# Cross attention: the negated maxima as two rows of the turned queries, by way of DRAM; gate logits with the gate as the stationary side

## The chip, the cores and the metric

The kernel runs on one core of a Trainium2 chip. The time is the device time of one execution, in microseconds. The engines are named as the profile names them: PE is TensorE (PEld its weight loads), DVE is VectorE, ACT is ScalarE, POOL is GpSimd, and SP issues most DMAs.

## What is computed

The program is one block of a model with two layers, for 4 batches of 512 tokens with 512 features (16 tiles of 128 tokens). The change lies in the second layer, in its cross attention and in the routing of its mixture of experts. Cut to those two:

```
# cross attention: 16 heads of 32 features, in 4 groups of 4 heads that share keys and values
scores = einsum('bghsd,bgtd->bghst', qh, kh) / sqrt(32)
probs  = softmax(scores, axis=-1)
out    = einsum('bghst,bgtd->bghsd', probs, vh)      # back to (b, s, 512)
x      = x + tanh(g_xattn[1]) * (out @ Wc.T + bc)
# mixture of experts: 8 experts, two for each token
gate_logits = einsum('bsd,de->bse', layernorm(x), gate_kernel)    # 512 -> 8, in f32
top_k_weights, top_k_indices = top_k(gate_logits, 2)
x = x + tanh(g_ffn[1]) * (weighted sum of the two experts)
```

The queries are the layer norm of x; the keys and values are both the context, 512 positions with 4 groups of 32 features.

## The kernel before

The kernel is written engine by engine: each engine has its list of instructions, and semaphores order them across engines. There is no scheduler. The stages follow one another: first attention, first feed-forward part, cross attention (functions with `_c`), routing (`_route`), experts (`_slots`).

**Cross attention.** It runs over 16 tiles `i` of 128 queries, and in each over 16 steps `s`; `k = 16 i + s`. A step does two different things for two different tiles.

- `scores(n)` makes the 128x512 scores of tile n // 16 and head n % 16, queries down and keys across, and DVE's `peak(n)` takes the maximum of each row. This runs ahead of the rest by `LEAD` = 24 steps.
- `scores_t(k)` makes the scores once more, turned: 128 keys down, 4 heads times 128 queries across, one product of 512 columns for group `g` and key block `c`. The maximum of each query has to be taken off before the exponential, and it varies across the columns here. So DVE's `split(i)` cuts the negated maxima into three bf16 parts in four small steps, PE's `mturn(i)` turns them, DVE's `spread_max(i)` spreads them into a tile `RM` of 128x512, and each `scores_t` begins with a product of a matrix `sel` of zeros and ones with `RM` into the same bank. ACT's `exps(k)` then makes the exponential into a ring of 12 buffers (`PT`).
- `values(k)`, two at every second step and four steps behind, multiplies by the values in f32, each call on 32 of PE's columns.
- POOL's `pool_sums` adds the exponentials of the four key blocks of a group, three additions for four steps, for the sums of the softmax.

The 32 features of a head fill only a quarter of PE's 128 rows. So the queries are laid out in four parts of 32 columns a head, two f16 high and two f16 low ones, and the keys too (`parts`, `twins`, `doubled`), which gives all four partial products in one matmul. `queries(i, half)` turns them on PE, ACT's `qcopy` copies them to `QTH`.

Behind the steps of tile `i` the previous tile is finished: `sums`, `sums_turn`, `spread_turn` (PE), `invert`, `normalise` (DVE), and `project` with 13 products. All of these, the query turns and `mturn` share PSUM bank 7, so their order on PE, and waits between them, keep them apart. Two banks (3 and 4) take the turned scores: `scores_t(k)` waits for the exponential of step k - 2.

**Routing.** For each of 16 tiles DVE normalises 512 features (`prep`), ACT makes their f16 high part (`high`), DVE the low one (`low`), PE turns the tile in four 128x128 f32 pieces (`turn`), ACT copies them (`zcopy`), and PE multiplies (`logits`): the stationary side is a turned piece of 128x128, the moving side 128x8 of the gate, four times a tile. There are two buffers of each kind, and the middle tiles run in a loop. Some fifty small steps of DVE on the logits follow, and then the experts. SP's loads of the first expert's weights wait for the first logits.

## Time and profile before

| | us |
|---|---|
| median of 3 runs | 1933.1 (1927.11 to 1937.12) |
| the profiled execution, its own time | 1933.01 |
| its span | 1931.2 |
| PE busy | 1554.0 (80%) |
| DVE busy | 1128.5 (58%) |
| ACT busy | 988.3 (51%) |
| POOL busy | 646.9 (33%) |
| PE's granted clock, mean | 0.893 of full |

The page cuts the span into 40 equal slices of 48.3 us, with the busy share of each engine and PE's granted clock in tenths. A table of windows gives the same for stretches of one's choice. The timeline gives each instruction, or a run of the same ones, with start, duration, line, operation and shape, and in square brackets how long the engine had been idle and who released it. A matmul's duration includes its way through the array; what it costs PE is the distance to the next one's start.

### The profile page before, as it was taken

The numbers are of one execution on the slowest core, as the hardware profiler recorded it, in microseconds if no ns is written. First come the engines' busy times: TensorE is split into PE (matmuls) and PEld (weight loads), VectorE is DVE, ScalarE is ACT, GpSimd is POOL, SyncE is SP. The second block draws the span as 40 slices with busy tenths as digits, with TensorE's granted clock in tenths as the row PEclk, the third lists the DMA queues.
The fourth block names the chain that finished last, engine by engine and source line by source line (L and its number), as shares of the span: only waits on it lengthen the run. The fifth ranks groups of instructions, "written<-read, shape, count | busy, mean of one in ns | idle before, by whom it ended". The sixth has DMA issues, their size and how long they took to land. (4 is left out here: it accounts for less than half of the span.)

```text
span 1931.2 us, 31926 instructions
## 1 busy us (share of the span) xinstructions
PE 1554.0 (80%) x10646; PEld 820.5 (42%) x10647; DVE 1128.5 (58%) x1845; ACT 988.3 (51%) x1487; POOL 646.9 (33%) x562
## 2 busy tenths in 40 slices
PE   6666565767677766999999780599999999999994
PEld 2444454533333332444444380244444444444442
DVE  3999999788888887777777354405145050522000
ACT  4999999522222224766766432144444443444442
POOL 3000000110000002777777606444445453444342
PEclk9777878788988887999999955799999999999998
DMA  9311100000000000000000036514255151532113
GB/s 333 122 44 44 44 1 1 28 1 0 0 0 0 0 1 1 2 2 2 2 2 2 18 136 256 201 34 122 64 163 163 33 158 27 163 79 51 28 24 102
DMA packets 48415, 118.45 MB, mean 61 GB/s; under 512 B 4736, under 2 KB 4992, under 8 KB 47744
## 3 DMA queue, kind: packets, MB, share of 16 engines
q1 hardware_dynamic: 34000, 88.26, 13.5%
q0 software_dynamic: 8176, 18.65, 5.0%
q10 hardware_dynamic: 6144, 10.28, 1.8%
q8 instruction: 58, 0.95, 0.2%
q14 instruction: 37, 0.30, 0.0%
HBM read 84.08 MB, written 37.30 MB: 63 GB/s over the span
## 5 line engine op out<-in xcount | busy, mean ns | idle before, releaser
L1608 PE MATMUL PS<-R 128*128 (+1 forms) x1872 | 432.8, 381 | 8.6 <-issue 7.5
L1762 DVE TENSOR_SCALAR R<-wring 128x1024 f16<-128x1024 f32 x56 | 61.4, 1107 | 383.0 <-PE PS L1631 349.5
L423 ACT ACTIVATE R<-R 128x512 bf16<-128x512 f32 x448 | 278.4, 710 | 9.9 <-DVE R L528 3.5
L1608 PEld LDWEIGHTS PS<-R 128*128 128x128 f16 x1872 | 179.3, 98 | 218.2 <-issue 20.4
L443 PE MATMUL PS<-R,ident_b 128*128 128x256 bf16 (+1 forms) x1056 | 161.6, 312 | 87.5 <-ACT R L423 83.6
L1631 PE MATMUL PS<-R 128*128 (+1 forms) x936 | 214.8, 379 | 1.2 <-ACT R L1718 1.2
L1023 DVE TENSOR_REDUCE R<-PS 128x1 f32<-128x512 f32 x256 | 167.8, 686 | 76.4 <-PE PS L1213 74.9
L1798 POOL TENSOR_TENSOR R<-R 128x512 f32<-128x512 f32 x78 | 113.5, 1456 | 292.4 <-ACT R L1706 181.1
L868 PE MATMUL PS<-R 128*128 128x512 bf16 x512 | 143.8, 433 | 77.1 <-DVE R L804 57.6
L1145 ACT ACTIVATE R<-PS 128x512 f32<-128x512 f32 x256 | 150.8, 597 | 86.3 <-PE PS L1228 85.2
L1000 POOL TENSOR_TENSOR R<-R 128x512 f32<-128x512 f32 x128 | 168.5, 1316 | 32.8 <-ACT R L1145 18.7
L443 PEld LDWEIGHTS PS<-R,ident_b 128*128 128x128 bf16 x1056 | 111.0, 117 | 116.8 <-ACT R L423 93.4
L321 POOL TENSOR_TENSOR rstd<-vare,mhalf 128x15 f32<-128x15 f32 (+1 forms) x8 | 13.2, 1658 | 365.1 <-DVE vare L308 337.4
L1631 PEld LDWEIGHTS PS<-R 128*128 128x128 f16 x936 | 89.9, 98 | 102.6 <-issue 1.4
L1806 POOL TENSOR_TENSOR R<-R 128x512 f16<-128x512 f32 x78 | 98.6, 1264 | 79.0 <-ACT R L1712 79.0
L626 POOL TENSOR_TENSOR R<-C,R 128x512 f16<-128x512 f32 x8 | 11.2, 1418 | 331.0 <-ACT R L621 331.0
L941 ACT ACTIVATE R<-PS 128x512 f32<-128x512 f32 x64 | 38.2, 597 | 159.8 <-PE PS L868 159.8
L1712 ACT CAST R<-R 128x512 f16<-128x512 f32 x78 | 48.2, 618 | 137.9 <-POOL R L1789 71.8
L1702 ACT ACTIVATE R<-PS 128x512 f32<-128x512 f32 x78 | 46.6, 597 | 140.0 <-PE PS L1608 140.0
L997 POOL TENSOR_TENSOR R<-R 128x512 f32<-128x512 f32 x64 | 89.5, 1398 | 79.6 <-ACT R L1145 77.9
L868 PEld LDWEIGHTS PS<-R 128*128 128x128 bf16 x512 | 52.3, 107 | 149.0 <-DVE R L804 79.6
L1718 ACT COPY R<-PS 128x1024 f16<-128x1024 f16 x78 | 79.0, 1012 | 58.3 <-PE PS L1620 58.3
(262 smaller groups left out, 2727.2 us busy)
## 6 DMA issues: line engine op xcount, KB each, us to landing
wring<-in_L_ffn_w_kernel_dram SPq DMA_DIRECT2D x48, 512.0 KB, 5.0
slot_rows<-R SPq DMA_DIRECT2D x1, 10023.0 KB, 40.1
R<-slot_rows ACTq DMA_DIRECT2D x39, 257.0 KB, 2.7
R<-in_L_ffn_w_kernel_dram SPq DMA_DIRECT2D x16, 512.0 KB, 6.0
wring<-in_L_ffn_wo_kernel_dram SPq DMA_DIRECT2D x16, 512.0 KB, 4.7
R<-in_L_ffn_wo_kernel_dram SPq DMA_DIRECT2D x16, 512.0 KB, 4.7
X<-in_x_dram SPq DMA_DIRECT2D x4, 1024.0 KB, 10.1
R<-in_L_ffn_w_up_dram SPq DMA_DIRECT2D x4, 1024.0 KB, 10.3
```

The lines of the kernel that those rows point to most:

```text
L423: nc.scalar.activation(marks[:, j * S:(j + 1) * S], SIM[:, tile * S:(tile + 1) * S], ACT.Sign, bias=cfloat[:, tile:tile + 1], scale=-1.0). ...
L443: mm = nc.tensor.matmul(bank[4 + h % 2][:, lo * 64:hi * 64], weight, marks.rearrange("p (t m) -> p t m", m=S)[:, lo:hi, c * 64:(c + 1) * 6 ...
L868: mm = nc.tensor.matmul(bank[2 * m + n], bzt[b][:, k * P:(k + 1) * P], WGU[:, col:col + 512], start=(k == 0), stop=(k == 3))
L997: nc.gpsimd.tensor_tensor(to, PT[u * 4 % RINGP], PT[(u * 4 + 1) % RINGP], ALU.add).then_inc(sx_step, 1)
L1000: nc.gpsimd.tensor_tensor(to, to, PT[(u * 4 + c) % RINGP], ALU.add).then_inc(sx_step if c == 2 else sx_done, 1)
L1023: nc.vector.tensor_reduce(cmx[:, n % NH:n % NH + 1], bank[n % 3], AX, ALU.max).then_inc(max_done, 1)
L1145: nc.scalar.activation(PT[k % RINGP], bank[3 + k % 2], ACT.Exp, scale=QK_SCALE).then_inc(exp_done, 1)
L1608: mm = nc.tensor.matmul(bank[2 * half + g], ZT[n][:, (4 * pz + k) * P:(4 * pz + k + 1) * P], weights(place, at), start=(i % 12 == 0), stop ...
L1631: mm = nc.tensor.matmul(bank[4], ITT[half][:, (4 * pz + c % 4) * P:(4 * pz + c % 4 + 1) * P], weights(place, at), start=(half == 0 and i = ...
L1718: nc.scalar.copy(ITT[half], bank[6 + half].bitcast(F16)).then_inc(itt_sb, 1)
L1798: nc.gpsimd.tensor_tensor(IT[half], SL[half], U[half], ALU.mult).then_inc(it32, 1)
L1806: nc.gpsimd.tensor_tensor(IL[half], IT[half], IH[half], ALU.subtract).then_inc(il_sb, 1)
```

## The change

**In the cross attention** the product with `sel` goes, and `sel`, `RM`, `mask` and `spread_max` with it. The negated maxima enter the scores themselves. The fourth part of the keys is now a constant: 8.0 in its first two columns and zeros elsewhere; the fourth part of the queries is zero. So `scores` sees three of the four partial products and nothing from part four. DVE's `split` makes -maximum/8 as an f16 high and an f16 low part, in two steps. PE's `mturn` turns those 32 columns, a new `max_copy` on ACT copies the 32x128 result, and a new `sp_maxima` on SP writes it to a small DRAM tensor and reads it back as 2 rows of 2048 into rows 96 and 97 of `QTH[i % 3]`, behind the last `scores` of that tile. `scores_t` then waits for that transfer in place of `rm_done` and is a single product.

`LEAD` becomes 28. The work around the steps is moved: query turns from s = 0, 2 to 1, 3, `mturn` from 10 to 5, `sums` from 4 to 6, `sums_turn` from 6 to 8, `spread_turn` from 8 to 10; `project` does 9 of its products at 13 and 4 at 15. ACT and DVE follow. DVE's subtraction for the query parts works on 512 columns instead of 1024. In the key preparation POOL does one subtraction a batch instead of two, and two fills once.

**In the routing** the gate is the stationary side, 128x32 (8 columns, the rest zeros), and a turned tile the moving side. Four tiles are done together, each on its own 32 of PE's columns; the 128x128 result, logits down and tokens across, is copied by DVE, turned back by PE (`back`), and after the last one DVE copies all logits at once. Buffers of each kind become four, and the loops are written out. POOL's tables and SP's expert loads wait for the first four tiles' logits instead of the first tile's.

```diff
-        LEAD, LAG, RINGP = 24, 4, 12
+        LEAD, LAG, RINGP = 28, 4, 12
+        KEY_ONE = 8.0
...
+        def sp_maxima(sp):
+            for i in range(NT):
+                sp.wait_ge(mq_sb, i + 1)
+                if i > 1:
+                    sp.wait_ge(max_in, (i - 1) * 16)
+                sp.dma_start(MD[i % 2][:, :], mq).then_inc(mq_out, 16)
+                sp.wait_ge(mq_out, (i + 1) * 16)
+                sp.dma_start(QTH[i % 3][96:98, :], MD[i % 2][:, :].rearrange("(n h) q -> n (h q)", n=2)).then_inc(max_in, 16)
...
-                nc.vector.tensor_tensor(twins(qs, 1), doubled(cz), twins(qs, 0), ALU.subtract).then_inc(qlo, 1)
+                nc.vector.tensor_tensor(parts(qs, 2), heads(cz), parts(qs, 0), ALU.subtract).then_inc(qlo, 1)
...
+            def max_copy(i):
+                act.wait_ge(mt_ps, i + 1)
+                if i:
+                    act.wait_ge(mq_out, i * 16)
+                nc.scalar.copy(mq, bank[7].bitcast(F16)[0:32, 0:P]).then_inc(mq_sb, 1)
...
             def scores_t(k):
                 i, g, c = k // NH, k % NH // 4, k % 4
-                pe.wait_ge(rm_done, i + 1)
+                pe.wait_ge(max_in, i * 16 + 16)
...
-                nc.tensor.matmul(to, sel[:, g * P:(g + 1) * P], RM[i % 2], start=True, stop=False)
-                nc.tensor.matmul(to, KTA[:, at:at + P], QTH[i % 3][:, g * 512:(g + 1) * 512], start=False,
+                nc.tensor.matmul(to, KTA[:, at:at + P], QTH[i % 3][:, g * 512:(g + 1) * 512], start=True,
                                  stop=True).then_inc(st_ps, 1)
...
                     if s == 13 and i:
-                        if i + 1 < NT:
-                            pe.wait_ge(rm_done, i + 2)
-                        else:
-                            pe.wait_ge(rcp_sb, i)
-                        project(i - 1)
+                        pe.wait_ge(rcp_sb, i)
+                        project(i - 1, ((0, 0), (0, 1)))
+                    if s == 15 and i:
+                        project(i - 1, ((1, 0),))
...
                 for k in range(4):
-                    mm = nc.tensor.matmul(bank[2 + b][:, 0:NE], dzt[b][:, k * P:(k + 1) * P],
-                                          GK[:, k * NE:(k + 1) * NE], start=(k == 0), stop=(k == 3))
+                    for j in range(4):
+                        mm = nc.tensor.matmul(bank[4 + q % 2][32 * j:32 * j + 32, 0:P], GK[:, k * 32:(k + 1) * 32],
+                                              dzt[j][:, k * P:(k + 1) * P], start=(k == 0), stop=(k == 3))
                 mm.then_inc(lg_ps, 1)
```

PE in a middle tile of the cross attention, steps 4 to 6 before. L1227 is the product with `sel`, L1228 the turned scores, L1213 the scores for the maxima, L1246 the sums, L1238 the values, L1252 a turn for the sums:

```order
L1227 MATMUL PS<-R 128x512
L1228 MATMUL PS<-R,wring 128x512
L1213 MATMUL PS<-wring,R 128x512
L1246 MATMUL PS<-R,ones 32x512 x4
L1227 MATMUL PS<-R 128x512
L1228 MATMUL PS<-R,wring 128x512
L1213 MATMUL PS<-wring,R 128x512
L1238 MATMUL PS<-R,C 32x128 x8
L1227 MATMUL PS<-R 128x512
L1228 MATMUL PS<-R,wring 128x512
L1213 MATMUL PS<-wring,R 128x512
L1252 MATMUL PS<-ident,R 128x128 x4
```

The same engine now, steps 5 to 8. L1232 is the turned scores, L1218 the scores for the maxima, L1242 the values, L1223 the turn of the maxima, L1250 the sums, L1256 the turn for the sums:

```order
L1242 MATMUL PS<-R,C 32x128 x8
L1223 MATMUL PS<-ident_h,R 32x128
L1232 MATMUL PS<-R,wring 128x512
L1218 MATMUL PS<-wring,R 128x512
L1250 MATMUL PS<-R,ones 32x512 x4
L1232 MATMUL PS<-R,wring 128x512
L1218 MATMUL PS<-wring,R 128x512
L1242 MATMUL PS<-R,C 32x128 x8
L1232 MATMUL PS<-R,wring 128x512
L1218 MATMUL PS<-wring,R 128x512
L1256 MATMUL PS<-ident,R 128x128 x4
```

A step has two products of 512 columns instead of three, and the turn of the maxima stands just ahead of the sums, which were at step 4.

PE in the routing before, the first tiles and the loop's body. L1527 is a tile's turn, L1535 its logits; the other rows belong to the loop:

```order
L1527 MATMUL PS<-ident,R 128x128 x8
L1535 MATMUL PS<-R 128x8 x4
L1542 UNCONDITIONAL_BRANCH
L1542 ISA
L1525 REGISTER_ALU
L1527 MATMUL PS<-ident,R 128x128 x4
L1531 REGISTER_ALU
L1535 MATMUL PS<-R 128x8 x4
```

The same place now; L1533 is the turns, L1542 the logits of four tiles, L1548 the turn back:

```order
L1533 MATMUL PS<-ident,R 128x128 x24
L1542 MATMUL PS<-R 32x128 x16
L1533 MATMUL PS<-ident,R 128x128 x12
L1548 MATMUL PS<-ident,R 128x128
L1533 MATMUL PS<-ident,R 128x128 x4
L1542 MATMUL PS<-R 32x128 x16
```

Six tiles' turns stand ahead of the first logits instead of two, and the logits come once for four tiles.

## Rows read from the trace of the kernel before

**Rows 1.** The page: busy tenths of PE and POOL, and PE's clock, in forty slices.
```profile
PE   6666565767677766999999780599999999999994
...
POOL 3000000110000002777777606444445453444342
PEclk9777878788988887999999955799999999999998
```

**Rows 2.** Table of windows: busy us (instructions) of each engine, PEclk, DMA share, GB/s.
```profile
775.00:1050.00 275.00, 274.27 (x2817) 129.05 (x2819) 208.48 (x343) 190.52 (x306) 207.44 (x154) 1.00 0.01 2
...
1110.00:1150.00 40.00, 39.53 (x192) 39.34 (x192) 20.70 (x47) 17.77 (x32) 2.21 (x9) 0.50 0.46 169
```

**Rows 3.** Timeline of PE, two steps: start, duration, line, operation, shapes, count.
```profile
882.18 0.38 PE L1227 MATMUL PS<-R 128*128 128x512 bf16 x1
882.39 0.38 PE L1228 MATMUL PS<-R,wring 128*128 128x512 f16 x1
...
882.92 0.64 PE L1238 MATMUL PS<-R,C 128*32 128x128 f32 x16
883.50 0.39 PE L1227 MATMUL PS<-R 128*128 128x512 bf16 x1
...
884.15 0.61 PE L1203 MATMUL PS<-ident_h,R 128*128 128x128 f16 x8
```

**Rows 4.** Timeline of PE: projections of two tiles, twelve tiles apart.
```profile
789.52 2.75 PE L1268 MATMUL PS<-R 128*128 128x512 f16 x12
...
1050.52 2.75 PE L1268 MATMUL PS<-R 128*128 128x512 f16 x12
```

**Rows 5.** Timeline of POOL: an addition held up, and two groups without a gap.
```profile
899.48 1.89 POOL L997 TENSOR_TENSOR R<-R 128x512 f32<-128x512 f32 x1 [1.12 <-ACT R L1145]
...
1074.83 2.69 POOL L1000 TENSOR_TENSOR R<-R 128x512 f32<-128x512 f32 x2 [2.25 <-ACT R L1145]
...
1079.06 2.69 POOL L1000 TENSOR_TENSOR R<-R 128x512 f32<-128x512 f32 x2
```

**Rows 6.** Timeline of ACT: a copy of half the turned queries, and two exponentials.
```profile
882.38 1.01 ACT L1138 COPY R<-PS 128x1024 f16<-128x1024 f16 x1
...
1074.15 1.09 ACT L1145 ACTIVATE R<-PS 128x512 f32<-128x512 f32 x2 [4.05 <-PE PS L1228]
```

**Rows 7.** Timeline of PE: the sums of the last tile.
```profile
1095.19 1.06 PE L1246 MATMUL PS<-R,ones 128*32 128x512 f32 x8 [1.66 <-POOL R L1000]
```

**Rows 8.** Timelines of PE, ACT and DVE at the start of the cross attention.
```profile
748.58 0.29 PE L1218 MATMUL PS<-ident_b,R 128*128 128x128 bf16 x1 [1.10 <-ACT R L1138]
...
753.11 0.63 PE L1227 MATMUL PS<-R 128*128 128x512 bf16 x1
...
748.42 1.24 ACT L1128 ACTIVATE R<-X,nmr,rstd 128x1024 f16<-128x1024 f32 x1
...
729.82 1.23 DVE L1017 TENSOR_TENSOR R<-R 128x1024 f16<-128x1024 f32 x1
```

**Rows 9.** The page, DMA issues: queue, count, KB each, us from issue to landing.
```profile
R<-in_L_xattn_Wq_dram SPq DMA_DIRECT2D x1, 64.0 KB, 5.8
...
R<-n_L_ffn_gate_kernel_dram ACTq DMA_DIRECT2D x1, 16.0 KB, 1.9
```

**Rows 10.** Timelines of PE, ACT and DVE in the routing.
```profile
1110.47 1.94 PE L1527 MATMUL PS<-ident,R 128*128 128x128 f32 x8 [3.87 <-DVE R L1389]
...
1113.96 1.09 PE L1527 MATMUL PS<-ident,R 128*128 128x128 f32 x4
1114.85 1.71 PE L1535 MATMUL PS<-R 128*128 128x8 f32 x8
1116.42 1.09 PE L1527 MATMUL PS<-ident,R 128*128 128x128 f32 x4
...
1115.84 0.58 ACT L1507 COPY R<-PS 128x512 f32<-128x512 f32 x1
...
1150.20 0.17 DVE L1400 COPY R<-PS 128x8 f32<-128x8 f32 x1 [1.54 <-PE PS L1535]
```

More of the change, by code:

```diff
@@ L1176, in act_c @@
             high(2)
+            max_copy(0)
             for i in range(NT):
@@ L1259, in spread_turn, with project @@
                 mm.then_inc(rst_ps, 1)
-            def project(i):
+            def project(i, parts):
                 pe.wait_ge(cot_hi, i + 1)
-                nc.tensor.matmul(bank[7], one_h, bch, start=True, stop=False)
-                for part, w in ((0, 0), (0, 1), (1, 0)):
+                if parts[0] == (0, 0):
+                    nc.tensor.matmul(bank[7], one_h, bch, start=True, stop=False)
+                for part, w in parts:
                     if part:
@@ L1396, in low @@
                                         ALU.subtract).then_inc(dlo, 1)
-            def logits(i, b):
-                v.wait_ge(lg_ps, i + 2)
-                nc.vector.tensor_copy(LG[:, bass.ds(i * NE, NE)], bank[2 + b][:, 0:NE]).then_inc(lg_sb, 1)
-            prep(0, 0)
-            prep(1, 1)
-            low(0, 0)
-            with v.Fori(0, NT // 2 - 1) as m:
-                for b in (1, 0):
-                    i = 2 * m + 2 - b
-                    prep(i + 1, 1 - b)
-                    low(i, b)
-                    logits(i - 1, 1 - b)
@@ L1411, in dve_route, with logits @@
-            low(NT - 1, 1)
-            logits(NT - 2, 0)
-            logits(NT - 1, 1)
+            def logits(q):
+                v.wait_ge(lg_ps, q + 2)
+                if q > 1:
+                    v.wait_ge(lgt_ps, q - 1)
+                nc.vector.tensor_copy(LT[q % 2], bank[4 + q % 2][:, 0:P]).then_inc(lt_sb, 1)
+            for t in range(4):
+                prep(t)
+            for t in range(NT):
+                low(t)
+                if t + 4 < NT:
+                    prep(t + 4)
+                if t % 4 == 2 and t > 4:
+                    logits(t // 4 - 1)
@@ L1415, in dve_route @@
+            logits(NT // 4 - 1)
+            v.wait_ge(lgt_ps, NT // 4)
+            nc.vector.tensor_copy(LG.rearrange("p (t e) -> p t e", e=NE),
+                                  bank[6].rearrange("p (t e) -> p t e", e=32)[:, :, 0:NE]).then_inc(lg_sb, 1)
             te = lambda ap: ap.rearrange("p (t e) -> p t e", e=NE)
@@ L1496, in act_route, with high, zcopy @@
             act.wait_ge(wct_ps, 4)
[L1497 removed]
+            act.wait_ge(gk_zero, 1)
+            act.dma_start(GK.rearrange("p (k e) -> p k e", e=32)[:, :, 0:NE],
                           gate_kernel.rearrange("(k p) e -> p k e", p=P)).then_inc(gk_in, 16)
[L1499 to L1516 removed]
+            def high(t):
+                act.wait_ge(dz_ready, t + 1)
+                nc.scalar.copy(ZHL[:, t * ROW:t * ROW + 512], dz[t % 4]).then_inc(dhi, 1)
+            def zcopy(t):
+                act.wait_ge(dzt_ps, t + 1)
+                if t > 3:
+                    act.wait_ge(lg_ps, t // 4 + 1)
+                nc.scalar.copy(dzt[t % 4], bank[t % 4]).then_inc(dzt_sb, 1)
+            high(0)
+            for t in range(NT):
+                if t + 1 < NT:
+                    high(t + 1)
+                zcopy(t)
             act.wait_ge(gap, 1)
@@ L1837, in _ @@
             sp_c(sp)
+            sp_maxima(sp)
             sp_x3(sp)
```

229 lines of the change are left out of this document (104 added, 125 removed).

## Prediction

> **What bounds the kernel now.** I read the page's forty slices first [rows 1]. Counted from one, slices 17 to 22 (772 to 1062 us) have PE and its clock at nine tenths or more; slice 24 (1110 to 1159 us) has PE at 8 but PEclk at 5. The first stretch is the cross attention, the second the routing, and the change touches both. The table of windows comes next [rows 2]: from 775 to 1050 us PE works 274.27 of 275 us at clock 1.00, while POOL has 207.44, DVE 208.48 and ACT 190.52. From 1110 to 1150 us PE works 39.53 of 40 us at clock 0.50, that is at 1.2 GHz, and DVE and ACT only about half of the time. So PE is the bound in both. Last, the timelines say what a piece of PE's work costs. A step of the cross attention without values takes 883.50 to 884.15 = 0.65 us, one with values 882.18 to 883.50 = 1.32 us [rows 3]. From one projection to the one twelve tiles later it is 1050.52 - 789.52 = 261.0 us, 21.75 us a tile [rows 4].
>
> **The spreading product goes.** It is the first matmul of a step: from its start to the next one's are 882.39 - 882.18 = 0.21 us, and a step without values is three equal products in 0.65 us, 0.216 each [rows 3]. There are 16 in a tile: 3.46 us. PE's own work of a tile falls to 21.75 - 3.46 = 18.3 us. Nothing on PE comes in its place but the small turn of the maxima, which was there before.
>
> **What is late next?** POOL's row sums. With nothing in its way POOL takes 1079.06 - 1074.83 = 4.23 us for the three additions of four steps [rows 5], 16.9 us a tile; an addition takes 1.27 us alone (two in 2.69) and 1.89 where DVE holds it up [rows 5], which brings a tile to some 17.5. That is under 18.3, so PE stays the bound where it has scores to make, but POOL is close. ACT: an exponential every 0.50 us (two took 1.09) and 1.01 us for a copy of half the turned queries [rows 6]; its 190.52 us in 275 us, 12.6 tiles, are 15.1 a tile [rows 2], and the copy of the maxima adds some 0.3: no bound on the mean. But the schedule puts its extras closer. I laid PE and ACT side by side for a tile by these rows. Behind the two query copies (s=1, s=3) the exponential of step 4 ends at about 5.7 us, and PE's scores of step 6, which need its bank, wait 0.3 us. The row sums at s=6 then wait 0.2 us for the copy of the maxima, queued on ACT behind the exponential of step 5; the projection waits 0.1 us for its operand. Together 0.55 us. DVE waits for nothing new that PE needs: it loses the spreading of the maxima and two of four small steps, and its halved subtraction. A tile takes 18.85 us. Bounds: none of these waits, 18.3; all twice and POOL's hold-ups on top, 19.9.
>
> **The maxima through DRAM.** Per tile one copy of 32x128 on ACT and two transfers in a row, one behind the other, on SP's queue. SP has nothing else there: the expert loads stand behind it and come after the cross attention in both kernels. The scores for the next tile's maxima end at s=3 (LEAD is 28, not 24), the copy ends about 6.4 us into the tile, and the first user is the next tile's first step, at 18.85. That leaves 12.4 us for two transfers. The trace has no such transfer; the nearest rows are the gate's 16 KB, landed in 1.9 us, and a 64 KB weight in 5.8 us at the start, in other traffic [rows 9]. I take 2.3 us each, near the first, as the queue is empty: hidden by 8 us. Even twice 5.8 us is hidden.
>
> **The first tile.** There is no cover here. Before, the maxima are turned at 748.58 and the first spreading product starts at 753.11, behind eight more scores; ACT's normalisation starts at 748.42 [rows 8]. Now DVE's part ahead of it is some 1.2 us shorter: a small reduction goes, and the subtraction (1.23 us on 1024 columns [rows 8]) does half. The turn of the maxima comes at about 747, but their copy stands behind that normalisation on ACT and ends at about 749.0. Two transfers of 2.3 us give 753.8; the twelve scores that now stand there, at DVE's 0.6 us each, end at about 753.5. So the first scores come some 1 us later than before: between 0 (transfers of 1.9 us) and 7 (5.8 us). The Trainium skill (DMA: Bandwidth & Descriptors, "Anatomy of one DMA") gives each DMA a fixed part of about 2 us, most of it the receipt of the write; by that the delay would be 0.3 us and the predicted time 0.7 us less. The gate's 1.9 us fits it, the 5.8 us does not.
>
> **The loop summed.** Before, from 753.11 to the last row sums at 1095.19 it is 342.1 us [rows 7, 8]. After: the first tile has no sums and no projection: eight steps of 0.65 - 0.22 and eight of 1.32 - 0.22 us are 12.3, the query turns and waits 1.5, together 13.8; twelve tiles of 18.85 are 226.2; the thirteenth to its projection 14.2 and its rest 4.3. The last two tiles have scores for 4 steps only, so PE would need 18.3 less 16 x 0.216 and less the query turns, some 14 us, for each, and POOL's 16.9 decides: 33.8 and 1.9 for its start and end, 35.7 us. Sum 294.2, 47.9 us less. Two of sixteen tiles thus save hardly anything, as POOL paced the last one before too.
>
> **The gate logits.** Before, on PE, a tile's turn takes 1114.85 - 1113.96 = 0.89 us and its logits 1116.42 - 1114.85 = 1.57 us, at 1.2 GHz [rows 10], though a product has 8 columns: the time is in the loads of 128 stationary columns, with PEld busy 39.34 of 40 us [rows 2]. From 1110.47 to DVE's last copy, done at 1150.37, it is 39.9 us [rows 10]. After, the gate is the stationary side, four tiles side by side on 32 columns each. That is the form of the values, where 8 such calls (16 entries) take 0.64 us at full clock, some 0.58 in a row [rows 3]: 16 calls 1.16 us, at half clock 2.3 us for four tiles. Four turns and one turn back are 3.8 us more. ACT must copy four turned tiles between one group's logits and the next's, since there are four buffers: a copy of 0.58 us [rows 10] and a cast like it, 1.1 us together, are 4.2 us for four, less one cast and with the wake-ups. So a group takes 4.2 + 2.3 + 0.2 = 6.7 us at half clock. The first logits end at 7.8 us, three groups more 27.9, copy, turn back and last copy 1.0: 28.9 us, 11 less. At full clock, with PE's times halved, a group takes 5.5 us and the whole 23.7, 16 less. The clock: the routing ran 40 us at 0.50 with PE all but full, on turns and short products [rows 2]; PE comes to it at half clock from the drain of the loop. After, products fill a third of PE's time. The Trainium skill (TensorE: Matmul & The Clock Gate, "PE-mode transpose") says that the full clock does not engage for transposes; by that the 11 us would be the whole gain and the predicted time 1875. The trace agrees as far as [rows 2] go. I take 12 us, near the end that the rows show. The expert loads start some 4 us later against the routing's start, and have over 30 us until they are used: nothing.
>
> **Costs at nothing.** One subtraction of the keys goes and two memsets come, once, under the end of the first attention, where POOL mostly sits idle [rows 1].
>
> **Sum.** The profiled execution took 1933.0 us, its span 1931.2; the median is 1933.1, so nothing is to be shifted. 1933.0 - 47.9 + 1 - 12 = **1874 us**.
>
> **The rivals.**
> (1) *A tighter pace*: no waits in the loop (18.3 us a tile, -6.6) and a shorter routing at mostly full clock: 1866 at the middle, down to 1862. For it: the step lengths are firm. Against: the stacked copies on ACT.
> (2) *POOL and ACT pace the loop*. For it: POOL's 16.9 us has 1.4 us of margin, and its additions that DVE holds up [rows 5]. A tile takes 19.9 us: 12.5 tiles x 1.05 = 13 us more, 1887.
> (3) *The clock falls*. In the last two tiles PE has 14 of 17 us to do. In slices 9 to 15 PE is 6 to 7 tenths busy and the clock 8 to 9 tenths [rows 1]. At half clock a tile is 28 us of PE; a third of two tiles gives +7: 1881, inside the range.
> (4) *The gate products do not pack*, so the change does not do what it says there: each of 16 calls takes 0.43 us alone, 6.9 us for four tiles, the routing stays at 40 us and more: 1888.
> (5) *The trip through DRAM is the bound: slower*. PE waits for it at each tile's first scores. It bites from 12.4 us for copy to landing, and takes back the whole gain of 59 us over 15 tiles at 3.9 us more, 16.3 us, over 8 us a transfer. At 9 us each it is +5.6 x 15 = 84: 1958. Against it: 1.9 and 5.8 us [rows 9], and DMA engines 1% busy there [rows 2].
>
> **How the numbers follow.** Forecast 0.56 (its own range 1867 to 1883), (1) 0.13, (2) 0.18, (3) 0.05 of its own, (4) 0.02, (5) 0.03, anything else near no change 0.03. The range takes in (1) to (4) and the bounds of the first tile: 1860 to 1896. Half a per cent, about what a measurement can tell, is 10 us: faster 0.94, same 0.03, slower 0.03.
>
> **What would show it.** Right: some 18.9 us from projection to projection, 16.9 in the last two tiles; PE at 97% there; the transfers landing 2 to 3 us each, long ahead of the first scores; the routing 29 us with clock 0.5. Wrong: gaps of PE released by POOL or by ACT above 1 us a tile, a clock under 1.0 in the loop, or PE waiting for a DMA anywhere but in the first tile.

## The result, and the profile after

The changed kernel takes 1873.4 us, median of 4 runs (1870.0 to 1877.0), against 1933.5 us of the kernel before in the same series: a ratio of 0.969 (95% interval 0.966 to 0.971), 60 us less. The forecast was 1874. The span of its profiled execution is 1868.7 us, 62.5 less than before.

The page of the changed kernel, the same lines as [rows 1]:

```profile
PE   6666666677776775999999711899999999999994
...
POOL 3000000010000000788888535435445444544432
PEclk9778777788898897999999765999999999999998
```

The block of nines on PE is six slices long on both pages, but a slice is now 46.7 us and not 48.3, and the block of nines on PEclk is one slice shorter. POOL has filled from 7 to 8 tenths under it. The three slices with clock 5, 5 and 7 behind it are now a 7, a 6 and a 5. The table of windows, to be laid beside [rows 2] (length, busy us of PE, PEld, DVE, ACT, POOL, with instructions, then PEclk, DMA share, GB/s), in the loop, in its end and in the routing:

```profile
775.00:1010.00 235.00, 227.99 (x2555) 109.58 (x2548) 198.47 (x298) 179.92 (x310) 198.19 (x151) 1.00 0.01 3
1010.00:1050.00 40.00, 34.82 (x416) 15.90 (x417) 15.31 (x27) 22.93 (x43) 36.16 (x28) 0.96 0.01 2
1072.00:1086.00 14.00, 8.17 (x111) 6.23 (x107) 12.48 (x23) 10.99 (x22) 2.90 (x9) 1.00 0.81 299
```

PE is still the fullest engine of the loop, but at 97% and no longer at 100%; DVE and POOL both stand at 84% (before 76 and 75). In the last two tiles POOL is the fullest, 36.16 of 40 us. The routing has changed character: clock 1.00 instead of 0.50, PE busy for 58% of the time, DVE for 89%.

PE's timeline, the sums of two middle tiles, eight apart, and of the last two, which answer to [rows 7] (start, duration, line, operation, shapes; in brackets how long PE had been idle, and for whom):

```profile
848.66 1.07 PE L1250 MATMUL PS<-R,ones 128*32 128x512 f32 x8
...
1000.95 1.06 PE L1250 MATMUL PS<-R,ones 128*32 128x512 f32 x8
...
1033.04 1.07 PE L1250 MATMUL PS<-R,ones 128*32 128x512 f32 x8
...
1049.15 1.94 PE L1250 MATMUL PS<-R,ones 128*32 128x512 f32 x8 [4.15 <-POOL R L1014]
```

From 848.66 to 1000.95 are eight tiles of 19.04 us, where there were 21.75. The last sums come 4.15 us after PE has run out of work, released by POOL, and take 1.94 us where they took 1.06 [rows 7]: the clock has fallen in that gap.

PE's timeline of the routing, the turns and the logits of its first group of four tiles, which answer to [rows 10]:

```profile
1065.74 5.35 PE L1533 MATMUL PS<-ident,R 128*128 128x128 f32 x24 [3.87 <-DVE R L1394]
1071.02 1.08 PE L1542 MATMUL PS<-R 128*32 128x128 f32 x32
```

And DVE's last copy of the logits:

```profile
1088.29 0.29 DVE L1419 COPY R<-PS 128x128 f32<-128x128 f32 x1 [0.46 <-PE PS L1548]
```

Twenty-four turns take 5.35 us, 0.22 each; 16 calls of logits with the gate as the stationary side (32 entries) take 1.08 us for four tiles. Before it was 1.57 us for one tile [rows 10].

**Where the 62.5 us went**, from the timelines of both kernels:

| stretch | before | after | difference |
|---|---|---|---|
| start to the first turned scores of cross attention | 753.1 | 751.8 | -1.3 |
| these to the last sums | 342.1 | 297.4 | -44.7 |
| last sums to the routing's first turn | 15.3 | 16.6 | +1.3 |
| first turn to DVE's last copy of logits | 39.9 | 22.8 | -17.1 |
| the rest | 780.8 | 780.1 | -0.7 |

The first row is mostly not the change's doing. DVE's last step ahead of the cross attention's queries stands at 724.72 us before and 722.53 after, with the first attention between, which differs by this much from one execution to the next (in another profiled execution of the same changed kernel, below, that step stands at 725.09). From there to the first turned scores it is 28.4 us before and 29.2 after: +0.85.

### The profile page after: what moved, and what is told of

It is laid out like the page before. It is cut to its first block and busy times, and to the rows that moved or that the text cites. A ratio compares the mean times of both kernels' runs of the same rounds, so it can differ in the third digit from the quotient of the medians.

```text
span 1868.7 us, 31243 instructions
## 1 busy us (share of the span) xinstructions
PE 1484.8 (79%) x10376; PEld 777.9 (42%) x10395; DVE 1112.7 (60%) x1785; ACT 980.8 (52%) x1503; POOL 635.6 (34%) x557
## 5 line engine op out<-in xcount | busy, mean ns | idle before, releaser
L445 PE MATMUL PS<-R,ident_b 128*128 128x256 bf16 (+1 forms) x1056 | 168.6, 321 | 83.1 <-ACT R L425 79.1
L1812 POOL TENSOR_TENSOR R<-R 128x512 f32<-128x512 f32 x78 | 113.3, 1453 | 292.0 <-ACT R L1720 181.0
L1036 DVE TENSOR_REDUCE R<-PS 128x1 f32<-128x512 f32 x256 | 166.6, 686 | 45.2 <-PE PS L1218 42.6
L1014 POOL TENSOR_TENSOR R<-R 128x512 f32<-128x512 f32 x128 | 166.6, 1302 | 27.8 <-ACT R L1141 12.2
L1141 ACT ACTIVATE R<-PS 128x512 f32<-128x512 f32 x256 | 144.4, 598 | 41.3 <-PE PS L1232 40.8
L445 PEld LDWEIGHTS PS<-R,ident_b 128*128 128x128 bf16 x1056 | 114.9, 120 | 114.6 <-ACT R L425 89.5
L944 ACT ACTIVATE R<-PS 128x512 f32<-128x512 f32 x64 | 38.2, 598 | 159.7 <-PE PS L871 159.6
L1726 ACT CAST R<-R 128x512 f16<-128x512 f32 x78 | 48.3, 619 | 137.7 <-POOL R L1803 71.6
L1716 ACT ACTIVATE R<-PS 128x512 f32<-128x512 f32 x78 | 46.6, 597 | 138.1 <-PE PS L1622 138.1
L627 POOL TENSOR_TENSOR R<-C,R 128x512 f16<-128x512 f32 x4 | 5.8, 1455 | 332.4 <-ACT R L623 332.4
L1218 PE MATMUL PS<-wring,R 128*128 128x512 f16 x256 | 100.4, 395 | 4.8 <-DVE R L1036 3.0
```

The lines of the kernel that those rows point to most:

```text
L445: mm = nc.tensor.matmul(bank[4 + h % 2][:, lo * 64:hi * 64], weight, marks.rearrange("p (t m) -> p t m", m=S)[:, lo:hi, c * 64:(c + 1) * 6 ...
L1014: nc.gpsimd.tensor_tensor(to, to, PT[(u * 4 + c) % RINGP], ALU.add).then_inc(sx_step if c == 2 else sx_done, 1)
L1036: nc.vector.tensor_reduce(cmx[:, n % NH:n % NH + 1], bank[n % 3], AX, ALU.max).then_inc(max_done, 1)
L1141: nc.scalar.activation(PT[k % RINGP], bank[3 + k % 2], ACT.Exp, scale=QK_SCALE).then_inc(exp_done, 1)
L1218: nc.tensor.matmul(bank[n % 3], QTH[i % 3][:, h * P:(h + 1) * P], KTA[:, at:at + 512], start=True, stop=True).then_inc(s_ps, 1)
L1812: nc.gpsimd.tensor_tensor(IT[half], SL[half], U[half], ALU.mult).then_inc(it32, 1)
```

## The experiments

Twelve kernels were run, one of them the changed kernel again. The kernel before was run beside them on each of three chips, with medians of 1936.4, 1935.9 and 1936.4 us.

### One half alone, and the other

The attention's part alone: all of the change but `pe_route`, `act_route`, `dve_route`, `pool_route_tables` and the routing's buffers.

```diff
-        GK = R2[:, 0:128]
-        dz = [R2[:, 512 + 512 * n:1024 + 512 * n] for n in range(4)]
+        GK = R2[:, 0:32]
+        dz = [R2[:, 512 + 512 * n:1024 + 512 * n] for n in range(2)]
...
```

> The changed cross attention with the routing of before. The theory that the two parts add up: the routing's 17 us come back, about 1890 us, ratio 0.978; the loop from first scores to the last sums 297 us as in the changed kernel, the routing 40 us at clock 0.50. Rival, that the routing's full clock came from the state in which the new loop left PE: the routing would be short here too, about 1875.

Measured: 1891.15 us (4 runs), ratio 0.976 (0.975 to 0.978), 45.2 us less. The loop has the same pace as with the whole change, and the routing the same 39.9 us as before. Its clock there, though it starts from the same drain as the changed kernel:

```profile
1066.00:1105.00 39.00, 37.38 (x182) 37.19 (x183) 21.00 (x48) 17.77 (x32) 2.73 (x10) 0.50 0.50 184
```

The routing's part alone, the same functions the other way round:

> The kernel before with the new routing alone. Adding up: 1933 - 17 = 1916 us, ratio 0.991, the clock in the routing rising to full some 5 us into it as in the changed kernel. Rival, that the clock depended on the new loop: the routing at half clock all along, 29 us for it, about 1922.

Measured: 1920.73 us (4 runs), ratio 0.991 (0.988 to 0.993), 15.6 us less. The two add up to 60.9 us, and the whole to 60.1 in its own series and 62.6 beside the kernel run again below. So the halves do not help or hinder each other by more than these 2 us or so, in which two series of the whole differ. The routing takes 24.1 us here (1113.82 to 1137.91), the clock in it rises and once falls back:

```profile
1124.96 1.08 PE L1539 MATMUL PS<-R 128*32 128x128 f32 x32
...
1130.57 1.94 PE L1539 MATMUL PS<-R 128*32 128x128 f32 x32
```

The same group of logits takes 1.08 us at the full clock and 1.94 at half of it. This falling back costs 1.3 us against the changed kernel's 22.8: from the group's turn back to the next it is 5.28 us (1129.43 to 1134.71), and 3.98 with the full clock (1081.35 to 1085.33 in the changed kernel). That is one group of four. The prediction put a group at 6.7 us at half clock and 5.5 at full, so both of its prices were too high, by 1.4 and 1.5 us in this place.

### What one product is worth

Each turned score product is issued twice, the second over the first, so that the step has as many products as before:

```diff
                 nc.tensor.matmul(to, KTA[:, at:at + P], QTH[i % 3][:, g * 512:(g + 1) * 512], start=True,
                                  stop=True)
+                nc.tensor.matmul(to, KTA[:, at:at + P], QTH[i % 3][:, g * 512:(g + 1) * 512], start=True,
+                                 stop=True)
```

> The changed kernel, but each product of the turned scores is made twice, the second over the first, so that a step has three products of 512 columns again; the maxima go through DRAM. If PE's third product is the whole of the loop's gain, a tile takes 19.04 + 3.46 less the waits that it covers (0.7) = 21.8 us, the kernel about 1873 + 40 = 1913. Rival, that part of the gain is the moved steps and DVE's shorter part: 21.0 us a tile, 1902.

Measured: 1909.5 us (one run), span 1907.7. PE's sums of two tiles, eight apart:

```profile
843.14 1.06 PE L1252 MATMUL PS<-R,ones 128*32 128x512 f32 x8
...
1015.25 1.06 PE L1252 MATMUL PS<-R,ones 128*32 128x512 f32 x8
```

A tile takes (1015.25 - 843.14) / 8 = 21.51 us, 2.47 more than without the second product, though 16 products are 3.46 us of PE. The window of this kernel says where the other microsecond is:

```profile
775.00:1000.00 225.00, 225.00 (x2333) 107.89 (x2325) 163.29 (x251) 158.17 (x264) 166.04 (x127) 1.00 0.01 3
```

PE is busy without a gap. So, as PE's own work alone sets this pace, the second product fills waits of 0.98 us a tile, and PE's own work in a tile of the changed kernel is 21.51 - 3.46 = 18.05 us. The product's removal is worth what PE's rows say, 3.46 us; 0.98 of it is given back in waits. The prediction had 18.3 and 0.55. The result lies between the two sides of the expectation (21.8 and 21.0 us a tile): against the 21.75 us of the kernel before, 0.24 us a tile of the loop's gain are not this product.

### The order of the projection and the residual

In the changed kernel the last of the three pieces of `project` stands at s=15, behind the others at s=13, and `residual` at s=15. Here the order of before is put back:

```diff
-                        project(i - 1, ((0, 0), (0, 1)))
-                    if s == 15 and i:
-                        project(i - 1, ((1, 0),))
+                        project(i - 1, ((0, 0), (0, 1), (1, 0)))
...
-                    if s == 15 and i:
+                    if s == 14 and i:
                         residual(i - 1)
```

> The changed kernel with the projection in one piece at step 13 and the residual at step 14, as before the change. By the waits in the trace (0.22 us a tile for the residual ahead of the query turns) a tile takes 18.8 us and the kernel 1870. Rival, that the split covers the copies stacked on ACT and DVE behind the projection: a tile 19.3 us or more, 1877.

Measured: 1889.25 us (4 runs), ratio 0.976 (0.974 to 0.977): some 16 us of the gain are gone, four times what the dearer side had (19.3 us a tile, and 4 us in all). A tile takes 20.18 us. DVE's timeline behind the projection:

```profile
908.15 0.69 DVE L1036 TENSOR_REDUCE R<-PS 128x1 f32<-128x512 f32 x1 [1.71 <-PE PS L1218]
908.76 1.67 DVE L1030 TENSOR_TENSOR R<-R 128x512 f16<-128x512 f32 x1
910.35 0.74 DVE L1066 SCALAR_TENSOR_TENSOR X<-PS,coef,X 128x512 f32<-128x512 f32 x1
```

And the waits of PE that this ends in:

```profile
911.14 0.62 PE L1208 MATMUL PS<-ident_h,R 128*128 128x128 f16 x8 [0.48 <-DVE X L1066]
912.55 0.38 PE L1218 MATMUL PS<-wring,R 128*128 128x512 f16 x1 [0.57 <-DVE R L1036]
```

DVE first sits idle for 1.71 us while PE does 12 products in a row and makes no scores; then it does its low part of the queries (L1030) and the residual, and PE waits for the residual, since the query turns want its PSUM bank. A third wait comes on top: the small step of 16 columns ahead of the turn of the maxima (L1042) now meets POOL's additions, takes 1254 ns on the mean instead of 544, and PE waits 0.38 us a tile for the step behind it (L1045). I had treated this move as one of order, worth nothing. It is worth 1.14 us a tile, the split and the later residual together, as this run puts both back: splitting a long run of products keeps the engines fed that live from the scores between them. How much of the 1.14 us is each of the two was not taken apart.

### POOL in the loop

One of each group's three additions is left out in all tiles: the second, that of the third key block, though the expectation calls it the third. The softmax sums then lack that block, so the kernel computes something else.

```diff
-                for c in range(1, 4):
+                for c in (1, 3):
...
-                        pool.wait_ge(sx_step, u * 2 + c - 1)
+                        pool.wait_ge(sx_step, u + 1)
```

> The changed kernel with the third addition of each group left out in all tiles (the softmax sums then lack one of four key blocks). If PE with its waits on ACT paces the middle tiles, they keep 19.0 us and only the last two shorten, 8 us in all: 1865. If POOL holds the middle tiles up as well, they fall to 18.5 or less: 1858.

Measured: 1861.5 us (one run), span 1859.7. The sums:

```profile
848.78 1.06 PE L1250 MATMUL PS<-R,ones 128*32 128x512 f32 x8
...
996.75 1.07 PE L1250 MATMUL PS<-R,ones 128*32 128x512 f32 x8
...
1040.77 1.06 PE L1250 MATMUL PS<-R,ones 128*32 128x512 f32 x8
```

A middle tile takes 18.50 us, 0.54 less, and from the sums of the thirteenth tile to the last it is 44.0 us instead of 48.2. The second was expected, since POOL paces the end. The first was not, because PE hardly ever waits for POOL in the middle tiles. The table of groups says how it comes about; of the changed kernel, DVE, 775 to 1010 us (busy us, mean ns):

```profile
L1030 DVE TENSOR_TENSOR R<-R 128x512 f16<-128x512 f32 x12 | 19.5, 1624 | 0.0
L1061 DVE TENSOR_TENSOR R<-R 128x512 f16<-128x512 f32 x13 | 18.9, 1453 | 0.0
L1057 DVE TENSOR_TENSOR R<-PS,R 128x512 f32<-128x512 f32 x13 | 8.8, 681 | 0.0
```

Of the kernel with two additions:

```profile
L1061 DVE TENSOR_TENSOR R<-R 128x512 f16<-128x512 f32 x13 | 8.9, 683 | 0.0
...
L1030 DVE TENSOR_TENSOR R<-R 128x512 f16<-128x512 f32 x12 | 8.2, 682 | 0.0
```

The same subtraction takes 682 ns with POOL out of its way and 1624 with it in its way. So DVE waits for POOL inside its instruction, the residual comes later, and with it PE's query turns. In the kernel with two additions PE's wait for the residual, 5.4 us in twelve tiles of the changed kernel, is gone from the table of waits, while the one for ACT's copy of the maxima stays (4.1 us against 3.8). So most or all of the 0.54 us, of the 0.98 us of waits in a tile, come by this path.

### The last two tiles

POOL paces them, with eight groups of 4.25 us on end. Here, from the fifteenth tile on, DVE adds the exponentials of two of the four key blocks, and POOL has two additions instead of three.

```diff
+                if i >= TAIL:
+                    ...
+                    nc.gpsimd.tensor_tensor(to, PT[u * 4 % RINGP], PT[(u * 4 + 1) % RINGP], ALU.add).then_inc(sx_step, 1)
+                    ...
+                    nc.gpsimd.tensor_tensor(to, to, PAIR[u % 2], ALU.add).then_inc(sx_done, 1)
+                    continue
...
+                    if i >= TAIL and s % 4 == 3:
+                        ...
+                        nc.vector.tensor_tensor(PAIR[u % 2], PT[(u * 4 + 2) % RINGP], PT[(u * 4 + 3) % RINGP], ALU.add).then_inc(pair, 1)
```

Beside it the changed kernel was run again, as the series' own standard:

> The changed kernel once more, to stand beside the next two on the same chip: 1873 us, ratio 0.969.

Measured: 1873.31 us (5 runs), ratio 0.967 (0.965 to 0.969). The tail on DVE:

> The changed kernel, but in the last two tiles of the cross attention DVE adds the third and fourth exponential of a group and POOL makes two additions a group instead of three. If POOL's 16.9 us a tile pace these tiles, as the page of the changed kernel says, POOL falls to 11.4 us a tile, PE with 14 us or ACT takes over: 5 us less in the two tiles and 3 us less of PE's wait ahead of the last sums, about 1865. Rival, that the chain from sums to projection over PE, ACT and DVE paces them anyway: no change, 1872.

Measured: 1873.96 us (5 runs), ratio 0.968 (0.967 to 0.969): no gain. The waits of the kernel from 1003 to 1052 us (in all, times, longest):

```profile
DVE R L1118 <- ACT R L1160: 17.7, 7, 3.0
POOL R L1015 <- DVE R L1118: 11.4, 8, 2.6
```

DVE's new addition waits for ACT's exponential, with everything queued behind it on DVE waiting too, and POOL waits for DVE. From the thirteenth sums to the last it is 47.15 us against 48.2. The load was taken from POOL and came back as a chain through three engines.

The same kernel with 32 products that nobody reads, put into PE's waits behind the last tile:

```diff
+            def warm(n):
+                for _ in range(n):
+                    nc.tensor.matmul(bank[0], KTA[:, 0:P], KTA[:, 0:512], start=True, stop=True)
+
+            pe.wait_ge(max_done, STEPS)
+            warm(6)
             sums(NT - 1)
+            warm(3)
             sums_turn(NT - 1)
+            warm(4)
             spread_turn(NT - 1)
             pe.wait_ge(rcp_sb, NT)
+            warm(7)
             project(NT - 1, ((0, 0), (0, 1), (1, 0)))
+            warm(12)
```

> As the one before, and PE is given products that nobody reads in the waits behind the last tile (6, 3, 4, 7 and 12 of 512 columns). The drain ran at half clock: its sums, turns and projection take some 3.5 us more than at full clock, and the routing's first turns 2.7 us more. If the clock stays up: 6 us less, about 1859. Rival, that the added products only stand in the way: 0 to 3 us more than the one before.

Measured: 1870.5 us (5 runs), ratio 0.967 (0.965 to 0.968), 3.5 less than its twin without them, where 6 were expected. The window from the last sums to the end of the drain, of this kernel, and the two windows of the changed kernel that it answers to:

```profile
1052.00:1065.00 13.00, 11.38 (x57) 4.62 (x55) 4.57 (x16) 2.40 (x4) 3.31 (x2) 1.00 0.15 50
```

```profile
1049.00:1057.00 8.00, 4.17 (x16) 1.67 (x16) 0.95 (x2) 2.40 (x4) 2.71 (x2) 0.50 0.01 3
1057.00:1065.00 8.00, 4.72 (x13) 1.60 (x13) 2.98 (x10) 0.01 (x1) 0.55 (x1) 0.71 0.21 66
```

The clock stays at 1.00, and from the last sums to the routing's first turn it is 13.1 us (1052.35 to 1065.47) against 15.3 of the twin. Its routing, 23.1 us, is 1.2 less than the twin's 24.3. Both together are 3.4 of the 3.5.

To see the clock apart from the tail, the changed kernel with the warm products alone, 16 in place of 6 ahead of the last sums:

> The changed kernel with 42 idle products (whose result nobody reads) put into TensorE's waits behind the last tile: 16 ahead of the last sums, 3 behind them, 4 behind their turns, 7 ahead of the last projection and 12 behind it. Theory (the 1.3 us that the stretch from the last sums to the routing's first turn became longer, 15.3 to 16.6 us, are the clock, which fell to half in the 4.15 us wait for GpSimd ahead of them): at full clock the last sums take 1.06 instead of 1.94 us, the eight turns 0.66 instead of 1.12 a group of four, the 12 products of the projection 2.75 instead of 4.33; the stretch becomes 13.1 us, as in the run with the tail on VectorE and warm products, and the routing keeps its 22.8 us, since it is no longer TensorE that sets it: 3.5 us less, 1870. Rival (that run's gain over its twin came from elsewhere, or the routing, started at full clock, loses it again in its waits for DMA or ScalarE): 1873, with the stretch at 13 us and the routing at 25 us or more.

Measured: 1872.65 us (5 runs, 1869.03 to 1873.53), ratio 0.967 (0.966 to 0.969). The drain does what the theory said:

```profile
1050.73 1.06 PE L1250 MATMUL PS<-R,ones 128*32 128x512 f32 x8 [0.47 <-POOL R L1014]
...
1063.86 1.94 PE L1544 MATMUL PS<-ident,R 128*128 128x128 f32 x16 [1.28 <-DVE R L1405]
```

It takes 13.1 us instead of 16.6, and the routing 23.1 instead of 22.8: 3.2 us less in these two stretches. The medians differ by 0.7 to 0.8 only. The profiled executions tell why: the first turned scores stand at 751.77, 754.32 and 753.51 us in the changed kernel, in its repetition and here, a scatter of 2.5 us from the stages ahead, as large as the gain. The gain in its stretch is shown; that the kernel as a whole is faster is not.

### The trip through DRAM

The maxima are sent through two scratch tensors in DRAM, four or ten transfers more, one behind the other:

```diff
                 sp.wait_ge(mq_out, (i + 1) * 16)
+                for h in range(4):
+                    sp.dma_start(MX[(h + 1) % 2][:, :], MX[h % 2][:, :] if h else MD[i % 2][:, :]).then_inc(hop, 16)
+                    sp.wait_ge(hop, (i * 4 + h + 1) * 16)
                 sp.dma_start(QTH[i % 3][96:98, :], ...
```

> The changed kernel with four more transfers of the maxima, DRAM to DRAM, one behind the other, ahead of the one to the queries. By the trace a transfer takes some 1.5 us with its waits and PE has 9 us of room in a middle tile: only the first tile is later, by 6 to 8 us, 1880. If the trip were already at the bound, each tile would be 6 us longer, 1960.

Measured: 1891.34 us (one run), where 1880 was expected. SP's timeline in a middle tile:

```profile
922.79 0.31 SPq L995 DMA_DIRECT2D max_parts<-R  x1
924.13 0.47 SPq L998 DMA_DIRECT2D max_hops<-max_parts  x1
926.08 4.63 SPq L998 DMA_DIRECT2D max_hops<-max_hops  x3
932.20 0.23 SPq L1000 DMA_DIRECT2D R<-max_parts  x1
```

The first transfer is back 1.34 us after its issue, the ones from DRAM to DRAM take 1.9 to 2.1 us each, and the sixth goes out 9.4 us behind the first. The pace of a middle tile is unchanged, 19.03 us: all six are hidden. Of the 18 us most lie at the start, where the first sums of the loop stand at 789.59 us instead of 773.04. Of these 16.6 us 4.1 come from the stages ahead (the first turn of the maxima stands at 749.04 us instead of 744.90), and most of the rest from two waits of PE, the first of them this:

```profile
761.85 0.61 PE L1237 MATMUL PS<-R,wring 128*128 128x512 f16 x1 [5.74 <-DMA R<-max_parts]
```

The first tile is covered only by its twelve scores, and the second, behind a first one of 13 us, has less cover than the others: PE waits another 5.61 us there.

> The same with ten more transfers. At 1.7 us each the trip takes 17 us more, 8 us over the room of a middle tile: 15 tiles x 8 = 120 us and 17 in the first tile, about 2010 us, slower than before the change; PE's waits would then be put down to the transfers and its clock would fall. If the transfers cost less than 1 us each they stay hidden: 1885.

Measured: 2088.04 us (one run), 152 slower than the kernel before. SP:

```profile
910.47 0.31 SPq L995 DMA_DIRECT2D max_parts<-R  x1
...
931.34 0.23 SPq L1000 DMA_DIRECT2D R<-max_parts  x1
```

PE's waits in the middle of it, and its window:

```profile
PEld PS L1237 <- DMA R<-max_parts: 159.8, 13, 17.8
```

```profile
800.00:1200.00 400.00, 256.25 (x2589) 120.20 (x2592) 207.42 (x300) 183.62 (x313) 196.38 (x150) 0.82 0.02 4
```

The twelve transfers span 20.9 us from the first's issue to the last's. This tile takes 30.8 us (to the next tile's first transfer, at 941.23), a tile on the mean of ten 32.0 (sums at 876.37 and 1196.44), and PE waits for the transfer once in each, 12.3 us on the mean and up to 17.8. In these waits the clock falls too, to 0.82 on the mean. So the fifth rival's mechanism is real and has the shape that the prediction gave it, hidden up to a point and then charged in full and more; it takes six times as many transfers as the change makes. The changed kernel's own:

```profile
905.74 0.30 SPq L993 DMA_DIRECT2D max_parts<-R  x1
907.08 0.23 SPq L995 DMA_DIRECT2D R<-max_parts  x1
```

Its first scores of the next tile start at 917.86, 10.8 us behind the second issue.

### What raises the clock in the routing

Of the 16 calls of logits in each group four are left, so that the turns stand nearly alone.

```diff
-                for k in range(4):
+                for k in range(1):
```

> The changed kernel with 4 of the 16 gate products of a group of four tiles (one of four feature blocks; the logits are then wrong in value and the routing is another). If the f32 products bring the full clock, it stays at 0.5 in the routing or rises much later; the routing is then 4 x 3.8 us of turns at half clock or more, 21 us. If the turns of 128 columns themselves bring it, the clock rises at the same 5 us and the routing takes 19 to 20 us at ACT's pace. The time of the whole says little, as other tokens go to other experts.

Measured: 1876.42 us (one run), span 1874.6. PE's timeline:

```profile
1067.68 5.36 PE L1533 MATMUL PS<-ident,R 128*128 128x128 f32 x24 [3.87 <-DVE R L1394]
1072.96 0.44 PE L1542 MATMUL PS<-R 128*32 128x128 f32 x8
```

The windows around it:

```profile
1067.60:1073.00 5.40, 5.32 (x28) 5.02 (x30) 5.12 (x10) 5.23 (x10) 0.00 (x0) 0.50 1.03 378
1073.00:1075.00 2.00, 1.58 (x17) 0.98 (x16) 1.81 (x4) 1.46 (x3) 1.35 (x4) 0.99 1.03 385
...
1080.00:1082.00 2.00, 2.00 (x10) 1.47 (x8) 1.81 (x4) 2.00 (x5) 0.00 (x0) 0.50 1.02 418
```

The clock goes from 0.50 to 0.99 behind the 24 turns, as in the changed kernel, with no product before it. So the turns alone bring it. The Trainium skill (TensorE: Matmul & The Clock Gate, "PE-mode transpose") says that the full clock does not engage for transposes; these runs show the contrary for turns of 128 columns in f32. The routing from first turn to last copy takes 22.6 us, not the 19 to 20 expected. With the old form, four turns and then a tile's four logits calls of 8 columns (eight entries) in alternation, it stays at 0.50 for 39 us (the window of the attention's part alone, above), though PE is as busy. So the form of the logits and the run of turns ahead of them are the candidates for what changed the clock; which of the two it is stays open, since no run had the long run of turns with the 8-column products behind it.

Second, the clock falls back at 1080, before the third group, and yet from first turn to last copy it is 22.6 us, no longer than with the changed kernel's 22.8. With PE's work this light, the stretch goes by DVE and ACT at either clock. With all sixteen products it does not quite: there a group at half clock costs between 0.2 us (5.34 instead of 5.16, the second group of the run with the projection in one piece, 1093.70 to 1099.04) and 1.3 us (above).

## Why the prediction was right, point by point

**What bounds the kernel.** Right. PE's work was the length of both stretches, and the time fell with it: 44.7 and 17.1 us. After the change this holds for the loop alone; in the routing DVE is busy for 89% of the time and PE for 58%.

**The spreading product.** 16 x 0.216 = 3.46 us a tile: right, shown by the run with the second product. PE's own work is 18.05 us and not 18.3. The difference of 0.25 I did not isolate; the turn of the maxima went from 128 to 32 columns and PE no longer waits for their spreading, which the prediction left at its old cost.

**Late next.** The waits were priced at 0.55 us a tile and are 0.98. The two errors nearly cancel: 19.04 us a tile against 18.85. What the prediction had missing is POOL's hold on DVE. It knew that DVE holds POOL up [rows 5] and charged it to POOL; it said of DVE that it "waits for nothing new that PE needs" and loses by "its halved subtraction". The subtraction halved did not get shorter: 1225 ns on 1024 columns [rows 8], 1624 ns on 512, because it now meets POOL's additions. The waits of PE in the changed kernel name its path, the residual (L1066), 5.4 us in twelve tiles, and the smaller one foreseen, the copy of the maxima (L1147):

```profile
PEld PS L1208 <- DVE X L1066: 5.4, 12, 0.5
...
PEld PS L1250 <- ACT R L1147: 3.8, 12, 0.3
```

**The maxima through DRAM.** Hidden, right. The room from the end of the copy was put at 12.4 us; in the trace the copy ends at 905.71 and the first scores that need it start at 917.86, 12.15 us. The transfers take less than the 2.3 us that were put in: the first is back within 1.34 us here, and of the sixteen in the kernel the slowest took 3.2 us to land. In the whole kernel the profile names a transfer twice as what PE waited for, 0.4 us in all.

**The first tile.** +1 forecast, +0.85 measured, but not for the reason given. This execution comes to the stage 2.2 us earlier (722.53 against 724.72), and seen from there the copy of the maxima was timed well: its end was put at 749.0, less 2.2 that is 746.8, and it ends at 746.83. The transfers were to decide, with their end at 753.8. They go out at 746.86 and 748.24, so the first took 1.38 us and not 2.3. The first turned scores, at 751.77, wait for the twelve scores ahead of them, which go at DVE's pace of 0.61 us each:

```profile
745.77 7.27 DVE L1036 TENSOR_REDUCE R<-PS 128x1 f32<-128x512 f32 x12 [3.48 <-PE PS L1218]
```

That is the second item of that sum (753.5, less 2.2 is 751.3). So neither 2.3 us nor the 2.0 that the Trainium skill (DMA: Bandwidth & Descriptors, "Anatomy of one DMA") gives for the fixed part of a transfer decided here. With 1.38 us to completion the trace does not agree with that figure, which that section gives for transfers issued by GpSimd, and SP issues these.

**The last two tiles.** 40.0 us from the thirteenth projection to the last sums forecast, 40.2 measured (1008.91 to 1049.15), and POOL paces them. The loop in all gained 44.7 us and not 47.9. Of the 3.2 us, 2.3 are the 0.19 us in twelve tiles; 0.2 are here, the rest is in the first tiles.

**Not foreseen: the drain, +1.3 us.** PE falls idle for 4.15 us ahead of the last sums, and the clock with it. The third rival had the clock falling in the last two tiles; it fell behind them, and costs 3.5 us against a full clock, 1.3 more than before.

**The gate logits: the term that was mis-sized.** -12 forecast, -17.1 measured. Two of its steps failed, the clock and the overlap. The clock: the prediction took that the routing would stay mostly at half, since it had run so before [rows 2] and came from the drain so, and put the full clock at 16 less. It came to the full clock in 5.3 us, after 24 turns in a row, which only exist because four buffers let PE run ahead by six tiles' turns. The overlap: a group was put at 6.7 us at half clock and 5.5 at full, a sum of PE's and ACT's times in a row, while part of them overlap; a group that ran at half clock took 5.3 us from turn back to turn back, and the same places of the changed kernel 5.16 and 3.98. No kernel with all its products ran this form at half clock from first to last. By the 0.2 to 1.3 us that a group lost by it, an estimate from the runs, three more groups at half clock (the first runs at half for 5.3 us in any case) would have cost 0.6 to 3.9 us, and not the 5.2 between 28.9 and 23.7. So the miss of 5.1 us is in part the clock and in part the overlap, and the shares stay open.

**The sum.** -44.7, +0.85, -17.1 and +1.3 are -59.7, and the measured medians differ by 60.1. The forecast of -58.9 was met because the loop gave 3.2 less, the drain 1.3 less and the routing 5.1 more. That the time came out within 1 us is luck: with one sign, these three would have put it 9.6 us off, outside the forecast's own 1867 to 1883 though not outside 1860 to 1896. Of the signs that were named for being right, the 18.9 us (19.04), the 97% and the transfers ahead of time came; POOL's 16.9 us a tile in the last two came too (four groups of 4.25), and the routing with clock 0.5 did not. Of the rivals, (4) and (5) are excluded as they stand; (2) names a part of what keeps the loop from 18.05 us, POOL and ACT, but above the forecast's own waits it cost 2.3 us and not 13; (3) came true in the drain only; (1) was right on the routing only.

## What to carry to other kernels

When an operation goes from the bounding engine, its price is its rows' distance, but the waits that it had covered come out: here 0.98 of 3.46 us a tile, and an order of the remaining products that splits the long runs, with a later residual, was worth 1.14 us a tile more. A round trip through DRAM costs nothing when it has half a tile of cover; in the first tile it costs what the work ahead does not cover: nothing of two transfers behind twelve scores, 5.74 us of six. Where a stretch sits at half clock with its engine full, a change of form can bring the clock up too: here it came up once four buffers let PE run ahead with turns and the products of 8 columns were gone. The clock is the smaller part of the 17.1 us, by the estimate above.

## What the hardware showed that I had not expected

- DVE and POOL block each other by whole instructions. A DVE subtraction with both inputs in SBUF takes 682 ns alone and 1624 on the mean beside POOL's additions; one that reads PSUM and SBUF (L1057) takes 681 in the same place, untouched. The Trainium skill (SBUF — State Buffer, "SBUF: two separate sides") describes this as a lock on a shared pair of ports, held for the whole instruction, and the rows agree. One case from the changed kernel, DVE and then POOL:

```profile
897.66 1.67 DVE L1030 TENSOR_TENSOR R<-R 128x512 f16<-128x512 f32 x1
```

```profile
897.51 2.96 POOL L1014 TENSOR_TENSOR R<-R 128x512 f32<-128x512 f32 x2 [0.16 <-ACT R L1141]
```

  DVE starts 0.15 us behind POOL's first addition and ends 1.67 us later, about that addition's 1.27 and its own 0.68; POOL's second addition ends 0.27 us later than it would have (2.96 against 2.69 for two).
- Even 16 columns are held up so: a DVE operation of 16 columns (L1045) that takes 175 ns elsewhere takes 1262 on the mean in the kernel with two additions, where it meets POOL. So that kernel did not free DVE of POOL everywhere: the meeting moved to this step.
- The granted clock rose from half (1.2 GHz) to full (2.4 GHz) behind 24 turns in a row, 5.3 us of them, with no other product between.
- Small transfers issued by SP (8 KB) are back in 1.34 us from SBUF to DRAM as a rule (median 1.3, the slowest 3.2 us to land), and in 1.9 to 2.1 us from DRAM to DRAM in a row of four.
